# A fifth PSUM bank in the rotation of the Q/K projection, and another order of jobs in the tail of a fused pre-norm transformer layer

## The reference

```
x = x + proj(causal_attention(layernorm(x) @ Wqkv + bqkv)) + bproj      16 heads of 64, scale 1/8
h = layernorm(x)
x = x + (h @ W.T + b) + (h @ V_r) @ C.T                                 V_r and C have rank 32
```

## Time and profile before

| | us |
|---|---|
| time, median of two runs | 896.0 (894.42 and 897.58) |
| the profiled execution, its own time | 894.34 |
| span of its slowest core (core 5), first to last instruction | 892.8 |
| spans of its other cores | 878.8 to 886.7 |
| PE busy on core 5 | 699.9 (78% of the span) |
| ACT, DVE, POOL busy on core 5 | 353.5, 281.3, 185.7 |

### The profile page before, as it was taken

The page is one execution under the profiler, slowest core; times in us unless marked ns, Lnnn a source line. Parts: engine busy times, 40 slices in busy tenths (PEclk is TensorE's granted clock), DMA queues, the critical chain, the costliest instruction groups (busy, mean ns, idle before and its releaser), DMA issues.

```text
span 892.8 us, 11459 instructions; the slowest of 8 cores (878.8 to 892.8 us)
## 1 busy us (share of the span) xinstructions
PE 699.9 (78%) x3433; PEld 296.4 (33%) x3433; DVE 281.3 (32%) x675; ACT 353.5 (40%) x769; POOL 185.7 (21%) x304
## 2 busy tenths in 40 slices
PE   0499999997168888888888897979797888855665
PEld 0244444443033333333333333323232333322222
DVE  2543434202025423344232323323223132243333
ACT  0141414140025554644656656465746667400000
POOL 2000000001025433342222324220222222213311
PEclk9999999999555557789989999889989988978888
DMA  8990200001930000010010100101000010111001
GB/s 163 211 204 21 75 21 23 1 1 24 166 93 1 1 1 25 1 47 29 20 48 1 48 24 24 48 1 48 1 25 24 1 48 1 48 48 47 24 23 48
DMA packets 15131, 38.18 MB, mean 43 GB/s; under 512 B 3401, under 2 KB 3425, under 8 KB 15073
## 3 DMA queue, kind: packets, MB, share of 16 engines
q0 software_dynamic: 7616, 11.67, 8.7%
q1 hardware_dynamic: 7457, 25.79, 8.4%
HBM read 39.68 MB, written 8.39 MB: 54 GB/s over the span
## 4 chain that ended last, share of the span: by engine, by line
PE 70%; DVE 9%; ACT 8%; issue 7%; DMA 4%; POOL 2%; DVEq 0%; SPq 0%; ACTq 0%; POOLq 0%
PE ps_pv L412 15%; PE ps_sp L428 9%; PE ps_w L543 7%; PE ps_sp L255 6%; PE ps_pv L255 6%; PE ps_u L428 4%; PE ps_w L612 4%; ACT xnt_a L435 4%; PE ps_bf L239 3%; PE ps_sp L282 3%; PE ps_w L282 3%; PE ps_pv L612 3%; ACT xf_a L435 3%; DMA xf_a<-wffn 2%; PE ps_w L591 1%
## 5 line engine op out<-in xcount | busy, mean ns | idle before, releaser
L435 ACT ACTIVATE xnt_a<-ps_sp 128x512 bf16<-128x512 f32 (+3 forms) x285 | 142.2, 540 | 149.2 <-PE ps_sp L428 113.2
L428 PE MATMUL ps_sp<-q_fm,k_fm 64*128 64x512 bf16 (+3 forms) x427 | 135.4, 397 | 44.0 <-ACT xnt_a L435 29.0
L442 POOL TENSOR_TENSOR xnt_a<-xnt_a,tri_sb 128x128 bf16<-128x128 bf16 x142 | 57.4, 425 | 261.1 <-ACT xnt_a L435 260.2
L412 PE MATMUL ps_pv<-xnt_a,v_on 128*66 128x512 bf16 (+3 forms) x356 | 110.3, 414 | 1.7 <-POOL xnt_a L442 1.3
L428 PE MATMUL ps_u<-q_fm,k_fm 64*128 64x512 bf16 (+2 forms) x213 | 85.6, 402 | 23.4 <-ACT xf_a L435 14.9
L435 ACT ACTIVATE xf_a<-ps_u 128x512 bf16<-128x512 f32 (+3 forms) x142 | 76.3, 537 | 52.9 <-PE ps_sp L428 43.7
L412 PE MATMUL ps_pv<-xf_a,v_on 128*66 128x512 bf16 (+3 forms) x284 | 90.7, 413 | 2.1 <-POOL xf_a L442 1.7
L435 ACT ACTIVATE xf_a<-ps_sp 128x512 bf16<-128x512 f32 (+3 forms) x142 | 71.0, 542 | 48.4 <-PE ps_sp L428 26.4
L442 POOL TENSOR_TENSOR xf_a<-xf_a,tri_sb 128x128 bf16<-128x128 bf16 x114 | 46.2, 425 | 145.4 <-ACT xf_a L435 144.1
L428 PEld LDWEIGHTS ps_sp<-q_fm,k_fm 64*128 64x128 bf16 x427 | 32.7, 95 | 129.3 <-issue 125.7
L481 DVE RECIPROCAL recips<-ps_bf 128x4 f32<-128x4 bf16 x64 | 11.7, 183 | 184.9 <-PE ps_bf L471 181.6
(11 more groups left out here) (73 smaller groups left out, 763.1 us busy)
## 6 DMA issues: line engine op xcount, KB each, us to landing
xf_a<-x SPq DMA_DIRECT2D x32, 512.0 KB, 4.0
y<-xf_a SPq DMA_DIRECT2D x16, 512.0 KB, 2.7
wq_a<-wqkv POOLq DMA_DIRECT2D x3, 2048.0 KB, 41.4
wq_a<-wproj POOLq DMA_DIRECT2D x1, 2048.0 KB, 19.9
xf_a<-wffn POOLq DMA_DIRECT2D x4, 512.0 KB, 26.6
bias_a<-bqkv POOLq DMA_DIRECT2D x1, 512.0 KB, 58.6
bias_a<-bffn POOLq DMA_DIRECT2D x1, 512.0 KB, 60.1
bias_a<-bproj SPq DMA_DIRECT2D x1, 512.0 KB, 9.2
```

Of the source, the lines that this page charges most:

```text
L412: e.matmul(ps_pv[hd][0:66, off * 128:512], v_on[:, ki2, 66 * hh:66 * hh + 66], chunk(cb)[:, 0:ncol], start=st, stop=sp),
L428: e.matmul(sbanks[sb][:, off * 128:512], k_fm[hp:hp + 64, hc, ki * 128:(ki + 1) * 128], q_fm[hp:hp + 64, hc, g * 512 + off * 128:(g + 1) * ...
L435: e.activation(chunk(cb)[:, 0:ncol], sbanks[sb][:, off * 128:512], AF.Exp, bias=0.0, scale=0.125),
L442: gate = P.op("pool", lambda e, cb=cb: e.tensor_tensor(chunk(cb)[:, 0:128], chunk(cb)[:, 0:128], tri01[:], ALU.mult), waits=[m_ex, m_cm], ...
```

## The change

Two edits. First, the Q/K groups of stage A rotate over five banks in place of four; the fifth is ps_u. 16 groups are one more than a multiple of five, so block 0 begins at bank 0, block 1 at bank 1, block 2 at bank 2, block 3 at bank 3. The attention's first use of ps_u now waits for the last reader of bank 4. Second, the tail's list of jobs is put in another order: b(0) and b(1) come after both a2 jobs of the pair of tiles, b(0) and c(0) before b(1) and c(1), and the same for tiles 2 and 3.

```diff
-        bank_reader = [None, None, None, None]
+        bank_reader = [None, None, None, None, m_bqkvT]
...
-        qkv_banks = [ps_s[0], ps_s[1], ps_pv[0], ps_pv[1]]
+        qkv_banks = [ps_s[0], ps_s[1], ps_pv[0], ps_pv[1], ps_u[:, 0:512]]
...
-                qkv_bank = (qkv_bank + 1) % 4
+                qkv_bank = (qkv_bank + 1) % 5
...
-        m_qkv_done = bank_reader[(qkv_bank - 1) % 4]
+        m_qkv_done = bank_reader[(qkv_bank - 1) % 5]
...
-        sb_reader = [bank_reader[0], bank_reader[1], m_bqkvT]
+        sb_reader = [bank_reader[0], bank_reader[1], bank_reader[4]]
...
-        tail = [("a1", 0), ("a2", 0), ("b", 0), ("a1", 1), ("a2", 1),
-                ("b", 1), ("c", 0), ("c", 1),
-                ("a1", 2), ("a2", 2), ("b", 2), ("a1", 3), ("a2", 3),
-                ("b", 3), ("c", 2), ("c", 3)]
+        tail = [("a1", 0), ("a2", 0), ("a1", 1), ("a2", 1),
+                ("b", 0), ("c", 0), ("b", 1), ("c", 1),
+                ("a1", 2), ("a2", 2), ("a1", 3), ("a2", 3),
+                ("b", 2), ("c", 2), ("b", 3), ("c", 3)]
```

## The result

| | us |
|---|---|
| time after, median | 899.0 |
| time before, median of the runs beside it | 895.9 |
| ratio after / before | 1.0034, 95% interval 1.0023 to 1.0045 |
| profiled execution: its own time, span of its slowest core (core 6) | 899.60, 898.1 |
| spans of its other cores | 882.6 to 893.8 |

The changed kernel is slower by 0.34%, some 3.0 us (0.0034 x 895.9; interval 2.1 to 4.0). That is within 2% and inside the range, but the forecast was +0.5 us. What follows is about the other 2.5 us.

What follows compares the result with a forecast made beforehand. PE was taken to bound the kernel (70% of the chain). 894.3 - 1.5 for the five banks + 2.0 for the tail = 894.8 us, or 896.5 on the median of the two runs shown; range 890 to 901.

Steps and rivals of the forecast that it cites:

- B: Tail: groups behind every stall still begin at 1.2 GHz, +2.6 us a pair, 899.7 us in all; chance 25%.
- gain 0, at most 0.1: Stage A, boundary into block 2: PE's two groups run 1.5 us sooner, then the transposes wait as long; gain in us.
- list of signs: What the profile should show: fewer V eviction waits, Wproj load 1.5 us earlier, a new tail stall of about 3 us.
- Term (1): Tail, last pair: the copy of tile 3's transposes directly follows the last statistics instruction on DVE, -1.82 us.
- Term (3): Tail, from tile 3's residual x2 to the copy of tile 2's transposes: +0.4 us (0.2 to 0.6).
- Term (5): Tail: tile 3's normalised tile and transposes now come behind c(2)'s last residual while PE stands still, +2.2 us (2.0 to 2.4).
- Term (2): Tail, projection of tile 3: a shorter stall ahead lets it run partly at full clock, -1.2 us.
- Term (6): Tail, c(3)'s multiplications: a longer stall ahead makes them run at the low clock, +1.4 us (0 to 1.4).
- Term (4): Tail, c(2)'s multiplications: the stall ahead is no shorter, so no change, 0 us (-1.4 to 0).
- Rival A: Tail: the clock holds through the shorter stall and c's multiplications run fast, -3.5 us a pair, 887.5 us; chance 15%.
- Rival C: Attention (stage B): starting 1.5 us earlier it may meet the clock otherwise, slowest core anywhere from 892 to 900; chance 10%.
- Rival D: Stage A: five banks do nothing, or their gain is eaten up at the weights' load, 898.0 us; chance 5%.

Runs made afterwards that it cites:

- e9_gap_fill: Kernel before the change with only the five banks added, plus six unread matmuls ahead of the first transposes after the boundary into block 2: ratio 0.9981.
- e5: Kernel before the change, old tail order, plus 16 unread matmuls in each of the two 5.7 us stalls of a pair: ratio 0.9906.
- e6: Kernel before the change with the new tail order, plus 12, 14 and 8 unread matmuls at three places in each pair: ratio 0.9947.
- e2_tail: Kernel before the change, still four banks, with only the new tail order: ratio 1.0035, tail 78.5 us.

## Why the prediction was right or wrong

**The time: right within its range, for a reason that was half right.** 899.0 lies in 890 to 901, and "within 2%" held. The forecast of +0.5 us was too low by 2.5 us. Of the rivals B came nearest in time (899.7), but by other terms than its own: it had W3 gain nothing, the tail 5.2 us longer and stage A 1.5 us shorter, where W3 did gain, the tail is 3.05 us longer and stage A 0.36 us shorter on average.

**Edit 1: the step that failed is "gain 0, at most 0.1" at the boundary into block 2.** The mechanism was seen: PE does its two groups sooner and stands as long before the transposes, and the third boundary gives its whole stall (1.6 us measured, 1.5 taken). What was missed is that before, two groups of matmuls lay between a wait of 1.84 us and one of 0.26 us, and after the change the idle time is one piece of 2.1 us. Behind that piece the clock falls on some cores, and 1.7 us go with it. The lower bound for that boundary should have been a loss. The PEclk rows show the fall itself; that the length of the stall decides it rests on the counts given with e9_gap_fill. That the 1.6 us of the third boundary pass on whole is not shown core by core: from the issue of the Wproj load to the first transposes of the feed-forward weight it took 21.8 to 23.9 us before and 21.0 to 23.7 us after. The prediction's own list of signs was also loosely worded: it spoke of two waits for the V eviction left, where its working and the profile have one.

**Edit 2, order: right.** Term (1), -1.82 for the copy: from the residual to the copy 3.05 in place of 5.04, -1.99. Term (3), +0.4: 5.39 in place of 5.04 on the last pair of core 6, with the transposes at the low clock. Term (5), +2.2 for the late b: 3.19 in place of 1.21, +1.98. The order by itself is neutral, as e5 and e6 show, and the terms (1), (3) at its lower end and (5) gave +0.4 for it.

**Edit 2, clock: two of the three terms right, one wrong.** Term (2), -1.2: W3 kept its clock wholly on three cores in the last pair (-2.46, x2-x2 7.7; in e2_tail, with the same tail, on six) and had lost it in the first pair everywhere (x2-x2 9.8 in place of 12.5; with the order's 2.0 taken off, -0.7). Averaged over cores and pairs x2-x2 fell by 3.08 (12.35 to 9.27), against 3.0 for (1) and (2) together. Term (6), +1.4, with (5): y-y rose by 3.5 us (7.12 to 10.64 on average) against 3.6. Term (4), "0", is the one that failed: x2-y rose by 1.1 us (12.43 to 13.51 on average), 0.4 of it term (3) and the rest clock. The low clock reached farther into the first multiplications of c than before, some 5 us in place of some 3, by the rows of the tail above. Why stays open. The transposes that now break up the stall ahead of them are not needed for it: two cores of e9_gap_fill, which has the old order, have x2-x2 11.5 and x2-y 13.55 in the first pair where the others have 12.4 to 12.6 and 12.4 to 12.5. The prediction had bounded this term by -1.4 to 0 on the ground that the stall was "no shorter"; it had no upper side at all, though its own rows had the clock fall at different points of a stall. Together the tail came out at +3.05 against +2.0, and stage A, averaged over the cores of the profile, at -0.36 (144.42 to 144.06) against -1.5: 1.05 + 1.1 = 2.2 of the missing 2.5 us.

**Rival A** (the clock holds, -3.5 a pair) was met only with fillers, and on one core: on core 6 of e6_fill_new the tail was 67.7 us. **Rival C**: the attention's length on the eight profiled cores ran from 556 to 572 us (from the first transposes of the feed-forward weight to the tail) before and from 556 to 573 after, so its scatter hides a few us in one execution, and only the many runs show the 3 us. **Rival D** was partly so: on the six cores of after on which the clock fell, edit 1 gives nothing. The Trainium skill, page "TensorE: Matmul & The Clock Gate", section "HAM oscillation — how this bites in real kernels", reports no further gain from PSUM double-buffering in one kernel. The rows of those six cores agree in the number, by another cause (the clock); those of the two other cores, 1.6 us shorter, do not.

## What to carry to other kernels

A wait that goes from one place often comes back at the next dependency of the same engine; ask then not only how long it is in total, but whether two short stalls with work between them have become one long one, for here the TensorE clock fell only behind the long one. When jobs of two tiles are put in another order for one engine in program order, write down for each queue what now stands behind what: here a win of 2.0 us ahead of one projection was paid back at the next tile, to 0.02 us in the last pair. Before moving an instruction on DVE, look at what POOL does in that microsecond.

## What the runs showed that was not expected

A stall of 2.1 us between full matmul work was enough for the granted clock to go from 1.00 to 0.50 on some cores and not on others (one, six, six and seven of eight in four profiles), with a price of 1.6 to 1.7 us; with 0.8 us left of it, on none. Before the change this place had 1.84 us and then matmuls, and no core fell. The page "TensorE: Matmul & The Clock Gate" of the Trainium skill, section "HAM oscillation — how this bites in real kernels", warns of idle gaps longer than this one. The measurement differs: here the shorter one cost.

DVE's normalisation of 128x1024 from float32 to bfloat16 took 0.81 us alone and 2.86 us when POOL's float32 add on SBUF began 0.02 us before it; POOL's add kept its 2.34 us, and the DVE instruction ended 0.54 us after it. Delaying POOL's start brought it back to 0.81. The Trainium skill, page "SBUF — State Buffer", section "Who interferes with whom", says that the two engines share a pair of ports, and that a DVE instruction of this kind, in a mode that uses both of DVE's ports, gets it only when an earlier GpSimd instruction is done. The rows agree in the order and roughly in the size: by that rule the end would be 0.81 us after POOL's, and it was 0.54.
